# A decoder layer on one core: the written-out order of all attention work is set anew

## The reference

```
def _layernorm(x): return (x - mean) / sqrt(var + 1e-5)
# block 1, 16 heads of 32 columns: every row attends to all 512 rows
q, k, v = ln @ wq.T + bq, ln @ wk.T + bk, ln @ wv.T + bv
x = x + softmax(q k^T / sqrt(32)) v @ wo.T + bo
# block 2, keys and values from the first 512 rows of ctx (128 columns wide): causal
q = ln(x) @ Wq.T;  k, v = split(ctx @ Wkv_expand.T)
x = x + softmax(causal(q k^T / sqrt(32))) v @ Wout.T
# block 3
x = x + gelu(ln(x) @ proj1.T + b1) @ proj2.T + b2      # 512 -> 2048 -> 512
```

## Time and profile before

| | |
|---|---|
| median of 3 runs | 1121.18 us |
| the profiled execution's own time | 1120.96 us |
| its span | 1119.2 us |
| TensorE (PE) busy | 1091.9 us, 98% |
| VectorE (DVE) busy | 677.4 us, 61% |
| ScalarE (ACT) busy | 477.3 us, 43% |
| GpSimd (POOL) busy | 455.9 us, 41% |
| granted TensorE clock, mean | 0.998 of full speed |

### The profile page before, as it was taken

One profiled execution on the slowest core, in us unless ns is written; L12 is line 12 of the kernel. 1 busy time (PEld: TensorE's weight loads), 2 busy tenths in 40 slices (PEclk: granted clock), 3 DMA queues, 4 the chain that ended last, 5 costly groups with the idle time before them and its releaser, 6 DMA issues.

```text
span 1119.2 us, 15758 instructions
## 1 busy us (share of the span) xinstructions
PE 1091.9 (98%) x5712; PEld 763.5 (68%) x5712; DVE 677.4 (61%) x1303; ACT 477.3 (43%) x792; POOL 455.9 (41%) x416
## 2 busy tenths in 40 slices
PE   6899999999999999999999999999999999999998
PEld 5656666666666655665666666658878887887887
DVE  6677776677667777778787787845543324224222
ACT  6365464556545755646555566551221111112110
POOL 1257444444556765555647577762010001001000
PEclk9999999999999999999999999999999999999999
DMA  8833442333334446345545445302201000001001
GB/s 278 268 108 114 120 130 76 95 114 94 105 102 147 122 133 174 109 128 163 153 128 176 133 145 179 95 1 85 94 19 38 1 1 37 0 0 38 1 1 38
DMA packets 73736, 110.29 MB, mean 99 GB/s; under 512 B 6976, under 2 KB 45888, under 8 KB 71744
## 3 DMA queue, kind: packets, MB, share of 16 engines
q1 hardware_dynamic: 70864, 102.00, 30.3%
q0 software_dynamic: 2080, 6.82, 2.1%
q10 hardware_dynamic: 720, 0.54, 0.1%
HBM read 71.58 MB, written 37.75 MB: 98 GB/s over the span
## 4 chain that ended last, share of the span: by engine, by line
PE 89%; POOL 4%; ACT 2%; DVE 2%; issue 1%; DMA 1%; SPq 0%; DVEq 0%; ACTq 0%; POOLq 0%
PE PS L1092 19%; PE PS L1093 18%; PE PS L1094 18%; PE PS L1231 12%; PE PS L1215 9%; PE PS L1198 9%; POOL P_sum L869 2%; PE PS L1218 1%; PE PS L1122 1%; PE PS L1226 1%; ACT PT L1010 1%; DMA stackK<-scratch 1%; ACT stackQ L992 1%; POOL oTL L858 1%; POOL P_sum L875 0%
## 5 line engine op out<-in xcount | busy, mean ns | idle before, releaser
L1010 ACT ACTIVATE PT<-PS 128x512 f32<-128x512 f32 (+1 forms) x432 | 228.8, 589 | 154.1 <-PE PS L1215 66.2
L869 POOL TENSOR_TENSOR P_sum<-PT 128x512 f32<-128x512 f32 x128 | 161.9, 1284 | 242.2 <-ACT PT L1010 234.8
L1453 DVE TENSOR_REDUCE m_cols<-PS 128x1 f32<-128x512 f32 x256 | 164.7, 684 | 60.3 <-PE PS L1198 59.6
L1198 PE MATMUL PS<-stackK,stackQ 96*128 96x512 f32 (+3 forms) x512 | 164.2, 378 | 4.9 <-ACT PT L1010 1.7
L1540 DVE CAST hidH<-hid 128x512 fp32r<-128x512 f32 x64 | 28.8, 450 | 224.6 <-ACT hid L1064 221.9
L1064 ACT ACTIVATE hid<-PS,b1c 128x512 f32<-128x512 f32 x64 | 44.0, 690 | 277.3 <-PE PS L1094 275.4
L1215 PE MATMUL PS<-stackQ,stackK 100*128 100x512 f32 (+3 forms) x512 | 160.1, 382 | 1.7 <-ACT stackQ L992 1.3
L875 POOL TENSOR_TENSOR P_sum<-P_sum,PT 128x512 f32<-128x512 f32 x112 | 141.8, 1288 | 6.6 <-ACT PT L1010 2.3
L1459 DVE CUSTOM_DVE_ANT_0 PS<-PS,mask_qk 128x128 f32<-128x128 f32 (+3 forms) x256 | 119.9, 517 | 37.9 <-PE PS L1198 37.8
L1467 DVE RECIPROCAL P_sum<-PS 128x512 f32<-128x512 f32 x32 | 107.4, 3357 | 47.5 <-PE PS L1231 47.0
L1215 PEld LDWEIGHTS PS<-stackQ,stackK 100*128 100x128 f32 x512 | 91.7, 191 | 55.0 <-ACT stackQ L992 25.2
(11 more groups left out here) (128 smaller groups left out, 1757.0 us busy)
## 6 DMA issues: line engine op xcount, KB each, us to landing
scratch<-stage SPq DMA_DIRECT2D x128, 256.0 KB, 2.9
stackK<-scratch SPq DMA_DIRECT2D x62, 256.0 KB, 3.9
stackQ<-scratch SPq DMA_DIRECT2D x46, 256.0 KB, 3.8
stackQ<-scratch SPq DMA_DIRECT2D x18, 512.0 KB, 4.8
stackK<-scratch SPq DMA_DIRECT2D x60, 128.0 KB, 4.1
stackQ<-scratch SPq DMA_DIRECT2D x28, 128.0 KB, 3.7
PT<-wT SPq DMA_DIRECT2D x3, 1024.0 KB, 8.8
x_res<-x SPq DMA_DIRECT2D x3, 1024.0 KB, 8.5
```

The costliest lines, as they stand in the source:

```text
L869: pool.tensor_tensor(P_sum[:, h, :], PT[:, h, :], PT[:, 4 + h, :], ALU.add).then_inc(p_added, 1)
L1010: nc.scalar.activation(PT[:, slot:slot + heads, q0:SEQ], PS[:, BANK["T", u, i], 0:heads * width].rearrange("p (h n) -> p h n", h=heads), A ...
L1198: mm = nc.tensor.matmul(dst[:, a, :], stackQ[0:STACK, par, h + a, q * P:(q + 1) * P], stackK[0:STACK, par, h + a, 0:n], start=a == 0, stop ...
L1453: nc.vector.tensor_reduce(m_cols[:, q, STACK + h:STACK + h + heads], bank, AX.X, ALU.max).then_inc(s_done, 1)
```

## The change

Only numbers in the tables are changed, and the sequences in `FILL`; no function is. The diff, cut to what is spoken of below (the other entries of `PLACES`, for all eight positions, change in the same way):

```diff
-FREED = dict(T=0.1, S=0.83, M=2.13, G=2.21, R=4.16, O=5.64)
+FREED = dict(T=0.43, S=1.05, M=3.69, G=1.94, R=3.72, O=5.42)
...
-RAW_PLACES = ((0, 0, 4.6, 9.94), (13.4, 23.38), (26.4,), (8.95, 27.39, 9.79, 15.95), (16.64,))
+RAW_PLACES = ((0, 0, 4.23, 13.45), (17.79, 23.4), (26.49,), (14.22, 30.43, 36.91, 18.58), (20.74,))
...
-CHUNK_PLACES = [(25, (2.64, 11.51)), (26, (11.73, 16.01)), (28, (6.82, 12.11)), (28, (16.39, 28.46)), (29, (11.77, 29.33)), (30, (11.24, 13.77))]
+CHUNK_PLACES = [(25, (0.33, 15.94)), (26, (6.48, 21.87)), (28, (7.96, 9.79)), (28, (19.82, 43.86)), (29, (13.48, 53.17)), (30, (7.98, 15.18))]
...
     CROSS, position 0
-                 scores=((0.0, 0.49), (2.49, 0.79), (5.33, 0.99), (7.52, 0.35)),
-                 values=(5.39, 6.03, 9.75, 15.01),
+             scores=((0.33, 0.12), (2.07, 0.43), (7.56, 0.27), (16.77, 3.07)),
+             values=(5.13, 5.98, 10.02, 23.34),
...
     CROSS, position 1
-                 scores=((0, 0.45), (2.57, 0.35), (5.39, 0.93), (8.07, 0.02)),
-                 values=(4.67, 5.0, 10.28, 15.74),
+             scores=((-34.32, 1.74), (-13.04, 2.98), (5.6, 0.12), (6.74, 13.26)),
+             values=(4.67, 4.84, 20.51, 30.59),
...
     CROSS, position 3
-                 scores=((0.39, 0.19), (2.13, 0.63), (5.91, 0.83), (10.48, 0.05)),
-                 values=(6.44, 7.89, 10.19, 15.56),
+             scores=((-14.54, 3.04), (1.21, 1.22), (5.9, 1.32), (8.62, -21.7)),
+             values=(7.24, 7.38, 13.4, 15.46),
...
-    CROSS: (('Q', 'K', ('Wo', 0), ('xT', 0), ('xT', 1), ('Wo', 1), ('xT', 2), ('xT', 3)),
-            ('Q', 'K', ('Wo', 3), ('Wo', 2), ('V', 1)),
-            ('Q', 'K', ('V', 0), ('V', 2)),
-            ('Q', ('V', 3), 'K')),
+    CROSS: (('Q', ('Wo', 1), 'K', ('xT', 0), ('V', 3), ('xT', 1), ('xT', 2), ('Wo', 0), ('xT', 3)),
+            (('Wo', 3), ('Wo', 2), 'K', 'Q'),
+            ('K', 'Q', ('V', 2)),
+            ('Q', ('V', 0), 'K', ('V', 1))),
```

More of the change, by code:

```diff
@@ new lines @@
+    SELF: (
+        dict(body=23.31,
+             sums=(0, 62.7),
+             adds=(-0.71, 7.68, -11.32),
+             low=4.91,
+             bo=21.23,
+             scores=((0.73, 0.47), (2.3, 0.17), (4.63, 0.72), (10.06, 1.48)),
+             values=(5.07, 5.11, 13.72, 17.91),
+             maxima=(3.99, 11.42, 21.96),
+             fill=(-1.67, 12.98, 24.06),
+             stats=20.78,
+             divide=-1.41,
+             output=3.65),
+        dict(body=22.44,
+             sums=(0, 41.56),
+             adds=(-11.66, 4.16, -2.21),
+             low=12.04,
+             bo=16.2,
+             scores=((-1.74, 0.48), (1.43, 0.32), (6.7, 0.78), (11.07, 1.87)),
+             values=(5.0, 5.09, 19.89, 32.6),
+             maxima=(4.47, 8.37, 19.26),
+             fill=(0.79, 6.76, 22.06),
+             stats=1.67,
+             divide=-1.12,
+             output=6.68),
+        dict(body=15.86,
+             sums=(0, 29.31),
+             adds=(0.22, 6.31, 11.88),
+             low=6.11,
+             bo=-2.9,
+             scores=((-3.02, 0.31), (0.57, 0.52), (6.17, 1.07), (10.19, 1.54)),
+             values=(6.09, 8.89, 16.37, 16.65),
+             maxima=(4.52, 8.14, 13.33),
+             fill=(-7.57, 6.53, 14.37),
+             stats=2.49,
+             divide=-1.72,
+             output=3.25),
+        dict(body=24.47,
+             sums=(0, 25.58),
+             adds=(0.57, -12.44, -8.58),
+             low=15.48,
+             bo=7.4,
+             scores=((-33.13, 2.1), (2.89, 0.5), (7.07, 1.12), (10.56, 0.73)),
+             values=(6.14, 6.56, 11.64, 20.0),
+             maxima=(8.08, 11.62, 17.92),
+             fill=(3.19, 8.99, 18.21),
+             stats=4.65,
+             divide=-20.67,
+             output=5.8),
+    ),
@@ new lines @@
+    CROSS: (
+        dict(body=20.76,
+             sums=(0, 29.26),
+             adds=(-8.44, -5.34, -4.58),
+             low=25.2,
+             bo=19.02,
+             scores=((0.33, 0.12), (2.07, 0.43), (7.56, 0.27), (16.77, 3.07)),
+             values=(5.13, 5.98, 10.02, 23.34),
+             maxima=(4.54, 10.33, 17.55),
+             fill=(-1.14, 12.51, 22.77),
+             stats=15.73,
+             divide=4.0,
+             output=2.82),
+        dict(body=17.6,
+             sums=(0, 35.61),
+             adds=(-2.2, 6.85, 4.66),
+             low=7.5,
+             bo=23.19,
+             scores=((-34.32, 1.74), (-13.04, 2.98), (5.6, 0.12), (6.74, 13.26)),
+             values=(4.67, 4.84, 20.51, 30.59),
+             maxima=(-5.85, 0.13, 12.31),
+             fill=(-7.91, 4.83, 13.69),
+             stats=7.72,
+             divide=-12.52,
+             output=0.4),
+        dict(body=10.86,
+             sums=(0, 39.93),
+             adds=(-20.9, -7.39, -11.7),
+             low=-2.15,
+             bo=20.19,
+             scores=((-6.68, 1.36), (0.55, 0.59), (5.73, 1.32), (8.92, -2.39)),
+             values=(2.95, 6.24, 19.18, 26.59),
+             maxima=(2.45, 6.23, 7.68),
+             fill=(4.12, 7.39, 10.8),
+             stats=5.95,
+             divide=-1.1,
+             output=5.05),
+        dict(body=24.36,
+             sums=(0, 26.17),
+             adds=(-16.43, -2.7, -18.39),
+             low=14.85,
+             bo=9.88,
+             scores=((-14.54, 3.04), (1.21, 1.22), (5.9, 1.32), (8.62, -21.7)),
+             values=(7.24, 7.38, 13.4, 15.46),
+             maxima=(1.5, 7.24, 13.37),
+             fill=(0.88, 4.96, 21.79),
+             stats=5.56,
+             divide=0.79,
+             output=5.12),
+    ),
@@ L239 @@
 }
 FILL = {
[L243 to L245 removed]
+    SELF: (('K', 'Q', ('Wo', 1), ('xT', 0), ('xT', 1), ('xT', 2), ('Wo', 0), ('xT', 3)),
+           ('Q', ('Wo', 2), 'K', ('Wo', 3)),
+           ('Q', 'K', ('V', 3), ('V', 0)),
            ('K', ('V', 1), ('V', 2), 'Q')),
[L247 to L250 removed]
+    CROSS: (('Q', ('Wo', 1), 'K', ('xT', 0), ('V', 3), ('xT', 1), ('xT', 2), ('Wo', 0), ('xT', 3)),
+           (('Wo', 3), ('Wo', 2), 'K', 'Q'),
+           ('K', 'Q', ('V', 2)),
+           ('Q', ('V', 0), 'K', ('V', 1))),
@@ L251 @@
 }
-PARTIAL = ((30, 7.12, 0), (30, 8.89, 1), (31, 9.81, 2))
+PARTIAL = ((30, 4.58, 0), (30, 10.48, 1), (31, 9.3, 2))
 def spread(items, first, last):
```

2 lines of the change are left out of this document (1 added, 1 removed).

## The result

After the change four runs took 1105.57 us in the median (1104.51 to 1105.82), before it 1120.98 on the same chip (four runs). The ratio is 0.9857, its 95% interval 0.9844 to 0.9869: 15.4 us less, give or take 1.4. The forecast was 1107.0. The profiled execution after took 1104.51 us, its span is 1102.7. The kernel's lines are moved by four: L1231 of before is L1235 here, L1198 is L1202, L1215 is L1219, L1226 is L1230, L1010 is L1014, L992 is L996, L1459 is L1463. In the rows of the experiments L1190 is the max product, L1207 the scores, L1223 `four_heads`, L1218 the turn, L1114 the transposes xT, for which ScalarE's L945 makes the input, and L1084 the first product of a fill piece; L1002 is ScalarE's exponential and L1451 (L1445 in self) VectorE's maximum.

What follows compares the result with a forecast made beforehand. TensorE, busy for 98% of the span, was taken as the bound, with some 14 us lost to waits. 1120.96 - 9.2 - 2.2 - 3.0 - 3.2 + 3.5 = 1106.9, predicted as 1107 us, range 1101 to 1117.

Steps and rivals of the forecast that it cites:

- A: Brackets, the entries and exits of `four_heads` calls: 28 fewer, all in cross, at 0.33 us each, -9.2 us.
- B: After the turn, the next unit's first scores wait for ScalarE's copy of the maxima; cover removes this, -2.2 us.
- C: Units 19, 23, 27: T2's scores hold a bank until a late exponential, TensorE idles; 1.0 us each goes, -3.0 us.
- D: Change from self to cross, unit 15: first max's wait for the `stackK` load and the lower clock go, -3.2 us.
- E: New waits, mainly where joined calls wait for the last exponential among them: +3.5 us, from -1 to +9.
- three even races: Cross positions 3, 2, 0: TensorE against VectorE's last maximum, GpSimd's last add, T2's exponential; up to 0.5, 0.4, 0.3 us each.
- the low end: New waits at -1 us: of 14 us lost to waits, some 3 are at uncounted places, as unit 14's start.
- 1: Rival: the waits only move; the bracket saving lands, the other savings come back as waits elsewhere; 1112 us, 20%.
- 2: Rival: VectorE bounds positions 2 and 3 of cross, where the turn waits for the maxima; 1114 us, 7%.
- 3: Rival: the change does nothing on the whole, new waits of about 14 + 3.5 us eat all of it; 1121 us, 4%.
- 4: Rival: slower, GpSimd's chain sets the unit, and a delay of S comes back in the next; 1126 us, 7%.

## Why the prediction was right, step by step

- **A, right.** The count is in the trace (131 and 103 groups of L1231 and L1235), and the price in the runs: 0.32 us a bracket by the medians when 23 were taken apart (0.38 by the profiled executions), 0.32 in units 17 and 21 with the values set side by side in before, and 0.30 in units 18, 22 and 26 for one bracket each. The Trainium skill, "TensorEngine Tiling (Array Packing)", section Key Properties, says that changing the tiling mode drains TensorE; the loss of 0.32 us on a way in and out agrees with that, and the page gives no price. That different banks and operands don't separate two calls is shown by v3 and S.
- **B, right in the trace.** No wait for the copy from 445 to 690 us, 2.2 us gone. It was never tried alone: where the values were set side by side in before, it went too, overlaid by new waits.
- **C, right in size, its reason too small.** The sum took 3.0. The whole entry of position 3 gave 4.6 us, of which the brackets are 2.6 and C some 2. In after units 19, 23 and 27 go from 17.04 to 16.21 with two brackets fewer and a V piece (0.70) more, which leaves 0.87 each, 2.6 in all. But I had named the held bank alone. Moving T2 gave nothing and moving the maxima cost 4.7; the entry pays as a whole.
- **D, the step that failed.** The sum took 3.2 for it. In the two profiled executions units 14 and 15 went from 41.5 to 38.6 us, which looks like it, but 1.5 of that is a fall of the clock seen in one of seven profiled executions with the old order there; against the usual 40.0 it is 1.4. The cause was wrong too. The distance was enough by itself to end the wait (the load moved back brought none), and so was the load of ctxT moved away, which I had priced at 0 as work of engines with room. Neither is where the time was: with the wait gone alone, the next one took its place. In after v1 waits there. Of the 1.4 us 1.2 came with the new self entries: with the old ones in after these two units take 39.8. What in them gives it stays open. The distance itself, which I had put at 11.6 us (the terms add up to 11.5), is 12.8 in after.
- **E, too high.** The new waits that the ledger finds in after are 0.28 us in each of units 19, 23 and 27 and 0.5 in unit 0 (by its end, with the slow start taken off, 0.2); in units 28 to 31 it has 1.8, but 2.2 in before. That is +0.9 for the 3.5 predicted. None of the three even races was lost where I had looked for it, at the turn and at S: VectorE starts unit 23's last maximum at 587.75 and reads it out at 588.40, and the turn starts at 588.60. VectorE's nearness does cost a little: 0.2 of unit 23's 0.28 us stand at its max products, where the weight load waits for it. What I had left to the low end did come: unit 1 takes 19.7 us for 21.2.
- **The rivals.** 1 is what happened when the values were moved in the old order, where 3 of 13 us came back; in the new order the list is empty from 445 to 690 us. 2 fell with the row of 16.08 in 16.20 us: VectorE keeps up by 0.2. It does become the bound where the places are a little off, as the turn's waits for m_cols in two of the kernels above show; so what the Trainium skill says ("TensorEngine Tiling (Array Packing)", section Performance Considerations) of the emptying of PSUM holds here as an edge, not as the state. 3 and 4 fell with the list of waits, where GpSimd's adds hold S once, 0.5 us, as they did before.

By the ledger, with the usual 3.0 us for the stretch of D in before: -9.2 (A), 7.4 to 2.7 from 450 to 735 us (B, C and E), 3.0 to 1.3 from 403 to 450, 3.2 to 1.75 from 60 to 100, and +0.5 in unit 0 make -16.5, against -15.4 measured, with 1.4 either way. The predicted -14.0 was off by less than its parts: D was too large by 1.8, E by 2.6 the other way, and the 1.5 us of unit 1 stood in no term. That the sum came within 1.4 us of the measured gain is in part luck.

What stays open: the self entries give 2.3 us by the traces (unit 15 ends at 445.1 with them taken back, at 442.8 in after) and 0.6 by the medians. These runs can't tell which is right. Nor was anything tried that changes only `FREED` or `CHUNK_PLACES`; their part is in no term of the sum.

## What to carry to other kernels

Where small products run side by side in the array, count how often the work enters and leaves that form, and price it from starts, not from busy times: TensorE was 98% busy before and after. In an order written out by hand a wait can be worth less than it shows: here one of 1.4 us and three of 0.56 were worth nothing when they were taken away alone. So ask which chain set the time, and try the edit alone, unit by unit, before adding it to a sum. The trace by unit then tells which parts of a mixed result to keep: a kernel that gained nothing held 4 us in nine of its units.

## What the runs showed of the hardware that I had not expected

The same code takes a different time from one execution to the next, at a few places. Around 14 to 18 us, where all of them issue the same projections, a full-size product took 0.43 us from start to start in 9 of the 14 profiled executions and 0.23 in the other 5: here after, then before, TensorE in the stretch.

```profile
15.00:20.00 5.00, 5.00 (x16) 3.90 (x16) 5.00 (x9) 4.00 (x8) 0.00 (x0) 0.66 0.63 203
```
```profile
15.00:20.00 5.00, 5.00 (x23) 4.02 (x22) 4.90 (x9) 4.45 (x9) 0.00 (x0) 1.00 0.59 215
```

It is 16 groups of products against 23 in 5 us, at a granted clock of 0.66 against 1.00, and over the same 24 steps costs 1.6 us here and 1.3 to 1.9 in the nine; TensorE had waited 8.6 us for its first operand and 1.8 for the next shortly before. Only four of the nine show the lower clock in this view (0.66 to 0.68). In the other five the products are as slow from the first one on, but the trace has no record of the clock before 16.6 to 18.0 us, and the view prints 1.00, as in this row of the kernel with T2 moved:

```profile
15.00:20.00 5.00, 5.00 (x18) 3.95 (x17) 4.64 (x9) 4.04 (x8) 0.00 (x0) 1.00 0.56 211
```

So a 1.00 there is read beside the steps between starts. In unit 15 the clock fell in one execution of the seven with the old order of units 14 and 15, and in two of the 14 it stood at 0.50 for 3.4 us from 36 or 37 us on, with steps of 0.43. A single profiled execution so carries some 1.5 us that belong to no edit, which is half of what D claimed.
